# Clearing the diagonal of the inversion's error by a mask on VectorE instead of taking the identity off it by a product on TensorE

## The reference

```python
def step(S, xs):
    qt, kt, vt, gt, bt = xs
    S = S * jnp.exp(gt)[..., None, None]
    kv = jnp.einsum('bhk,bhkv->bhv', kt, S)
    delta = (vt - kv) * bt[..., None]
    S = S + jnp.einsum('bhk,bhv->bhkv', kt, delta)
    o = jnp.einsum('bhk,bhkv->bhv', qt * scale, S)
    return (S, o)
```

## Time and profile before

| | |
|---|---|
| median of 3 runs | 4421.18 us |
| the profiled execution | 4421.92 us |
| its span (first to last instruction) | 4420.1 us |
| mean granted clock of TensorE | 0.994 |
| PE matmul busy | 4348.0 us, 98% |
| DVE busy | 2558.0 us, 58% |
| ACT busy | 2348.6 us, 53% |
| POOL busy | 1306.0 us, 30% |

### The profile page before, as it was taken

One profiled execution on the slowest core, in us unless ns is written; L12 is line 12 of the kernel. 1 busy time (PEld: TensorE's weight loads), 2 busy tenths in 40 slices (PEclk: granted clock), 3 DMA queues, 4 the chain that ended last, 5 costly groups with the idle time before them and its releaser, 6 DMA issues.

```text
span 4420.1 us, 77500 instructions
## 1 busy us (share of the span) xinstructions
PE 4348.0 (98%) x28720; PEld 2987.7 (68%) x28720; DVE 2558.0 (58%) x5514; ACT 2348.6 (53%) x5915; POOL 1306.0 (30%) x1414
## 2 busy tenths in 40 slices
PE   8999999999899999999999999999999999999998
PEld 4444444444577777777777777777777777777776
DVE  4322222220366666666767776666667776676674
ACT  1111111110366666666666766666666676676675
POOL 1000000000123333333333333334344334443344
PEclk9999999999999999999999999999999999999999
DMA  4000000000200000000000011011111111111111
GB/s 142 30 26 24 30 11 30 28 14 25 93 20 21 23 21 23 21 21 28 23 21 21 25 40 61 23 54 35 42 35 45 35 37 37 35 44 37 35 35 42
DMA packets 108759, 154.13 MB, mean 35 GB/s; under 512 B 31841, under 2 KB 49249, under 8 KB 108385
## 3 DMA queue, kind: packets, MB, share of 16 engines
q1 hardware_dynamic: 72288, 93.94, 6.3%
q10 hardware_dynamic: 36096, 55.24, 4.0%
HBM read 113.73 MB, written 35.42 MB: 34 GB/s over the span
## 4 chain that ended last, share of the span: by engine, by line
PE 69%; DVE 1%; ACT 1%; POOL 1%; issue 1%; POOLq 0%; ACTq 0%; DVEq 0%
PE bank L958 20%; PE bank L1255 10%; PE bank L962 10%; PE bank L1532 10%; PE bank L1440 3%; PE bank L1426 2%; PE bank L1466 2%; PE bank L1401 2%; PE bank L1378 2%; PE bank L1154 1%; PE bank L1091 1%; PE bank L1155 1%; PE bank L1517 1%; PE bank L1007 1%; PE bank L1048 1%
## 5 line engine op out<-in xcount | busy, mean ns | idle before, releaser
L958 PE MATMUL bank<-xtile,wt 128*128 128x259 f32 x4096 | 1095.3, 394 | 21.1 <-DVE vraw L988 15.8
L958 PEld LDWEIGHTS bank<-xtile,wt 128*128 128x128 f32 x4096 | 723.0, 192 | 142.5 <-DVE vraw L988 45.4
L1312 ACT ACTIVATE xyinv<-bank 128x512 f16<-128x512 f32 x768 | 453.3, 593 | 276.4 <-PE bank L1255 273.6
L1532 PE MATMUL bank<-wot,xnt 128*128 128x512 f32 x1024 | 542.8, 620 | 0.8 <-ACT xnt L1525 0.8
L962 PE MATMUL bank<-wt,xtile 128*128 128x512 f32 x1024 | 524.5, 615 | 0.0
L1288 DVE TENSOR_TENSOR wlev<-bank,mask 128x256 f16<-128x256 f32 x768 | 317.1, 419 | 294.0 <-PE bank L1255 289.2
L988 DVE SCALAR_TENSOR_TENSOR vraw<-bank,taps,vraw 128x256 f32<-128x256 f32 x768 | 368.8, 480 | 62.2 <-ACT vraw L981 44.2
L1221 POOL TENSOR_TENSOR ltl<-ltm,lth 128x512 f16<-128x512 f32 x128 | 149.2, 1166 | 766.0 <-ACT lth L1215 766.0
L435 DVE TENSOR_TENSOR hid<-bank,gate 128x512 f32<-128x512 f32 x88 | 60.9, 692 | 490.2 <-PE bank L417 490.2
L1207 POOL TENSOR_TENSOR ltm<-ltm,mask 128x512 f32<-128x512 f32 x128 | 159.1, 1243 | 604.8 <-DVE ltm L1195 604.8
L412 PE MATMUL bank<-h2t,wt 128*128 128x512 f32 x704 | 325.4, 606 | 0.8 <-DVE h2t L387 0.8
(11 more groups left out here) (180 smaller groups left out, 8635.5 us busy)
## 6 DMA issues: line engine op xcount, KB each, us to landing
grows<-row_scratch ACTq DMA_DIRECT2D x126, 256.0 KB, 3.2
xtile<-xt_scratch ACTq DMA_DIRECT2D x30, 518.0 KB, 3.8
xn<-x SPq DMA_DIRECT2D x32, 256.0 KB, 5.5
xt_scratch<-xt SPq DMA_DIRECT2D x8, 1024.0 KB, 5.8
g_scratch<-sel SPq DMA_DIRECT2D x32, 256.0 KB, 2.0
part_scratch<-prow SPq DMA_DIRECT2D x32, 256.0 KB, 2.0
prow<-part_scratch SPq DMA_DIRECT2D x32, 256.0 KB, 2.6
sel<-g_scratch SPq DMA_DIRECT2D x32, 256.0 KB, 2.9
```

Source lines behind the costliest of these rows:

```text
L958: j = pe.matmul(b_p[:, 0:WIN], wt[:, k, c:c + P], xtile[:, par, k, :], **st)
L1312: act.activation(dst, b_inv[p][:].rearrange("p (a h b s) -> p a h b s", a=2, h=HEADS, s=z), ACT.Copy).then_inc(s[f"xy_sb{p}"], 1)
L1532: i = pe.matmul(b_o[:], xnt[:, h], wot[:, h], start=(h == 0), stop=(h == GV - 1))
```

## The change

A sixth mask M_OFF is added: one minus the identity, f16. The identity product goes out of `error`, so that the error bank now holds the error plus 64 times the identity. ACT and DVE split it into `errh` and `errl` as before. Then a second DVE instruction, behind a wait on DVE's own semaphore, multiplies `errh` in place by the mask, which sets its diagonal to zero. `el_sb` is now raised twice per unit. The table of times is changed for the two `error` steps, and with it the order on all engines.

```diff
-M_LT, M_LE, M_ID, M_NEG, M_L0T, M_EVEN = range(6)
+M_LT, M_LE, M_ID, M_NEG, M_L0T, M_OFF, M_EVEN = range(7)
...
+    m[:, M_OFF] = 1.0 - np.eye(P)
...
-        ident16 = mask[:, M_ID, :]
...
             pe.wait_ge(s["ltl_sb"], n + 1)
-            each_head(pe, b_inv[p], lambda h: ident16, lambda h: mask[:, M_NEG, :], stop=False)
-            each_head(pe, b_inv[p], lambda h: lth[:, p, h], lambda h: xyinv[:, p, 0, h], start=False, stop=False)
+            each_head(pe, b_inv[p], lambda h: lth[:, p, h], lambda h: xyinv[:, p, 0, h], stop=False)
             each_head(pe, b_inv[p], lambda h: ltl[:, p, h], lambda h: xyinv[:, p, 0, h], f"er_ps{p}", start=False)
...
                 act.wait_ge(s[f"c3_ps{1 - p}"], (n - 1) // 2 + 1)
-                act.wait_ge(s["el_sb"], n)
+                act.wait_ge(s["el_sb"], 2 * n)
...
             dve.tensor_tensor(errl[:], quad(b_inv[n % 2]), errh[:], ALU.subtract).then_inc(s["el_sb"], 1)
+            dve.wait_ge(s["el_sb"], 2 * n + 1)
+            dve.tensor_tensor(errh[:], errh[:], mask[:, M_OFF, :].unsqueeze(1).broadcast_to([P, HEADS, P]), ALU.mult).then_inc(s["el_sb"], 1)
...
-            pe.wait_ge(s["el_sb"], n + 1)
+            pe.wait_ge(s["el_sb"], 2 * (n + 1))
...
-            ("pe", "error"): 0.68
+            ("pe", "error"): 0.46
...
-            ("dve", "error"): 0.70
+            ("dve", "error"): 1.12
```

More of the change, by code:

```diff
@@ L1716, in attention @@
             ("dve", "conv"): 0.50, ("dve", "keys"): 0.70, ("dve", "gate"): 0.50, ("dve", "scores"): 0.70, ("dve", "decay"): 1.22, ("dve", "lower"): 0.69, ("dve", "attend"): 0.69,
-            ("dve", "start"): 0.42, ("dve", "level"): 0.42, ("dve", "error"): 0.70, ("dve", "second"): 0.69, ("dve", "third"): 0.69,
+            ("dve", "start"): 0.42, ("dve", "level"): 0.42, ("dve", "error"): 1.12, ("dve", "second"): 0.69, ("dve", "third"): 0.69,
             ("dve", "recall"): 1.13, ("dve", "learn"): 1.13, ("dve", "answer"): 0.87, ("dve", "out"): 0.70,
```

## The result

The changed kernel takes **4469.63 us** (median of 4 runs, 4468.69 to 4471.58) against 4422.07 us for the kernel before (4 runs beside it). The ratio is 1.0108, 95% interval 1.0092 to 1.0124: 47.6 us slower. The prediction was 4404, faster, with a range up to 4424.

A forecast was written before the change was run, and what follows sets the result against it. PE was taken to bound the kernel. From the profiled 4421.9 us, 28.9 came off for the product, 6 were added for the moved order and 5 for the mask's blocking, giving 4404; range 4390 to 4424.

The forecast's parts named there:

- What bounds the kernel: In the attention, PE at 98% busy sets the time; a microsecond taken from it comes off the end.
- The product, -28.9: Four identity matmuls a unit leave PE's error step: 128 x 0.226 = 28.9 us off, bounds 28.2 to 30.7.
- If the order on PE had stayed, it would fit.: Between errl and `first`, 0.46 us of mask was said to fit into 0.56 us of slack.
- 13 tight places: Units 24, 28, 40, 44 and so on, `error` to `first`: short by 0.33 us, up to 0.8 more behind POOL.
- What the mask really takes, +5: DVE's mask, blocked behind POOL, can take 1.2 us instead of 0.43: 5 us in all, bounds 0 to 14.
- What moves, +6: The changed order makes PE wait at hand-overs: net 0.8 us in four tiles, 6 us in all, at most 32.
- first to second value product, 6 times 1.07: On PE, 1.23 us of work where 2.3 is needed between the two products: short by 1.07 us, 6 times.
- That place is gone: Old order's one stall in four tiles, two levels behind two merges, about 1.5 us with the product behind, disappears.
- The meeting with POOL: Mask waits while POOL runs: by the skill's rule about 10 us beyond slack, sum 4409; rival 4417, chance 0.18.
- The slower rival: Mask on PE's path at every unit, losing 0.36 us each, 46 us against 28.9 gained: 4440 us, chance 0.13.
- The signs in the profile: Tiles of 100.3 to 101.0 us, some 7 us more idle ahead of feature products, over 15 ahead of `xyinv,errh` meaning slower.

The follow-up runs named there:

- e4: Kernel before in its old order, without identity product or mask, diagonal left in the error (a price only): 4401.55 us, ratio 0.9962.
- e3: Changed kernel in its new order with neither identity product nor mask, diagonal left in the error (a price only): 4445.43 us, ratio 1.0062.
- e2: Kernel before, identity product kept and no mask, with the changed table of times and so the new order: 4467.09 us, ratio 1.0112.
- e1: Changed kernel (mask, no identity product) with the kernel before's table of times and so the old order: 4463.38 us, ratio 1.0100.
- e5: Changed kernel in the old order, its mask instruction reading the error from PSUM instead of from errh: 4431.32 us, ratio 1.0018.
- e8: Changed kernel with the mask reading the error from PSUM and 13 table entries picked for it: 4418.35 us, ratio 0.9989.
- e6: Changed kernel with ACT's norm squares and its emptying of feature product 11's bank exchanged in 18 tiles: 4487.08 us, ratio 1.0144.
- e16: Kernel before with one unrelated table entry changed, ACT's merge step 0.58 instead of 0.61: 4495.27 us, ratio 1.0164.

## Why the prediction was wrong

- **What bounds the kernel** was right: PE, with no gap to spare. The stall column, which follows the times to within 9 us, says the same.
- **The product, -28.9.** Right as occupancy: the distance between starts in the traces is 0.223 to 0.224 us a unit, 28.6 in all. In time it gives 17 to 22 us (e4, and e3 against e2). 2.4 to 2.8 us come back as stalls. In e4 some 6 us are the clock (mean 0.993 over its runs, 0.995 over before's beside it); the remainder is within the intervals.
- **"If the order on PE had stayed, it would fit."** Wrong, and shown by e1: +61.8 us. The sentence set 0.46 us of mask against 0.56 us of slack. Three paragraphs later the text gave the mask 1.2 us behind POOL and counted 76 meetings, and then applied that only to the changed order's 13 tight places. The slack was too large as well: it was read with the product still there, and without it 0.34 us are left. 1.30 against 0.34 loses 0.96 at a unit that has the work of the earlier trace rows in between.
- **What the mask really takes, +5.** Undersized: +20.9 in the new order. The 13 places were the right ones, all of them stalled, by 0.9 us each (mask 1107 ns) where 0.33 and up to 0.8 were written. But 25 more places stalled too, 23.9 us in all ahead of `first` by the distances between starts. The steps behind the mask on DVE cost PE nothing more in this order: it waits 8.5 us for `wlev` in after and 8.3 in e3 without the mask.
- **What moves, +6: the step that failed.** It measured +48.4 with the program of before and +43.9 with neither. The prediction laid only PE's list against what each hand-over needs, with ACT, DVE and POOL ready at once. The place that it named (first to second value product, 6 times 1.07) was real, but it stalls in 21 tiles by 1.3 us, since ACT's list had moved as well, and stood waiting for POOL. Even its bound of 32 us was too low. "That place is gone" was right and worth less than written: the stalls ahead of levels fell from 11.9 to 6.1 us, not by 1.5 in each of seven stretches.
- **The meeting with POOL** was weighed as a correction of 5 to 10 us. In the old order it is worth about 36 us (e1 against e5). That masks are blocked behind POOL's large instructions shows in every run with two SBUF inputs, and that none is with one input in e5 and e8.
- **The slower rival** (4440, chance 0.13) had the side right and not the mechanism: PE waited for the mask at 26 units, not at each. The rival that mattered, a picked order given up, wasn't on the list.
- **The signs in the profile** were good ones: more than 15 us of waiting for `errh` was to mean the slower rival (16.4); 7 us more ahead of feature products was forecast, and 26.2 came; tiles took 102.6 us and not 100.3 to 101.0. The last was measured from the wrong mark, since the mean of four tiles before is 100.7 and not 101.2.

What stays open: which of the moved steps on which list makes the new order's loss. Its largest place is known, with some 25 of its 46 us (the second value product); e6 shows that it isn't the one exchange in which it surfaces. Other forms of the mask (earlier on DVE, or with POOL's ltl held back) weren't tried.

## What to carry to other kernels

Where a table of costs sets the order of a full engine, an edit to it is a change of its own: run the new instructions in the old order and the old instructions in the new one before you judge either, and move an unrelated entry by a little to see what a new deal costs by itself. If that alone costs more than the change can give, compare best table with best table. Work taken off the full engine ahead of a hand-over doesn't give the hand-over more time where another engine was already the one to wait for: here `errh` came no sooner. Look at the granted clock as well before a loss is put down to waits alone. And an instruction of DVE with two SBUF inputs is to be priced by what POOL does beside it, at all units and not in the median.

## What the runs showed of the hardware

- **A small POOL instruction doesn't block.** Masks that began during POOL's L1506 took their free 424 ns, 9 of 9 in e1, though L1506 reads SBUF too, 4 elements a partition. Timeline of e1:

```profile
2511.74 1.01 POOL L1506 TENSOR_TENSOR rms<-rms,mhalf 128x4 f32<-128x4 f32 x1
2512.29 0.42 DVE L1333 TENSOR_TENSOR errh<-errh,mask 128x512 f16<-128x512 f16 x1
```

- **The blocking goes both ways.** POOL's first step of the keys' norm, 8 elements a partition, had 304 ns in the median before, and 1161 after. Where it began with nothing beside it, or beside a DVE instruction with one SBUF input (L1282, L1288), it took 252 or 253 ns, once each; the 304 come from 27 starts inside L1276, which reads two. The source views of before and of after, and after's timeline, where it starts 0.07 us behind DVE's scan and ends 0.05 after it:

```profile
L1034 POOL TENSOR_SCALAR rnk<-rnk x32: 247/304/775, 1175.4 to 4269.6; 128x8 f32<-128x8 f32 x32
```

```profile
L1035 POOL TENSOR_SCALAR rnk<-rnk x32: 248/1161/1163, 1176.2 to 4312.6; 128x8 f32<-128x8 f32 x32
```

```profile
2349.30 1.18 DVE L1171 TENSOR_TENSOR_SCAN gam<-grows,mask 128x512 f32<-128x512 f32 x1
2349.37 1.16 POOL L1035 TENSOR_SCALAR rnk<-rnk 128x8 f32<-128x8 f32 x1 [2.61 <-ACT tsq L1021]
```

- **An instruction of ACT or DVE that doesn't wait starts sooner than the one ahead is said to end.** In e1's stretch above ACT's errh starts at 2476.04 and takes 0.60, and the next starts at 2476.52: 0.48 later. On DVE the start comes up to 0.09 us ahead of that end, as behind 127 of e1's 128 L1162. A planner's entry of 0.61 for errh overstates what it occupies.
- **Long waits of PE and a lower granted clock came together.** e6 (0.990 to 0.992) and e16 (0.989 to 0.990) are the only kernels with executions under 0.992, and in e6 the lower level of 1.2 GHz followed 8 of 12 waits of 2.0 to 3.3 us for `wlev`. Most of e16's followed shorter ones, of 1.01 and then 0.75 us. What decides it isn't shown here.
